# Second-weight remainder loads of a routed feed-forward stage: issued by ScalarE in two halves, instead of by SyncE in four quarters

## The reference

```python
router_probs = softmax(x_flat @ router_w.T)
top_k_probs, top_k_idx = top_k(router_probs, 2)
for e in range(8):
    h = new_gelu(x_flat @ w1[e].T + b1[e])      # 256 -> 1024
    out_e = h @ w2[e].T + b2[e]                 # 1024 -> 256
    output = output + cw[:, e:e + 1] * out_e    # cw: the two weights of a row
```

## Time and profile before

| | |
|---|---|
| median of three executions | 1002.55 us |
| the profiled execution's own time | 1003.09 us |
| its span, first to last instruction | 1001.0 us |
| TensorE matmul busy | 919.7 us (92%) |
| VectorE, ScalarE, GpSimd busy | 574.2, 588.3, 634.2 us |
| mean granted TensorE clock | 0.973 of full speed |
| loads of `w_remainder` | 168 of 256 KB, issued by SyncE |

### The profile page before, as it was taken

One profiled execution on the slowest core, in us unless ns is written; L12 is line 12 of the kernel. 1 busy time (PEld: TensorE's weight loads), 2 busy tenths in 40 slices (PEclk: granted clock), 3 DMA queues, 4 the chain that ended last, 5 costly groups with the idle time before them and its releaser, 6 DMA issues. The chain is left out here.

```text
span 1001.0 us, 21138 instructions
## 1 busy us (share of the span) xinstructions
PE 919.7 (92%) x6800; PEld 838.8 (84%) x6800; DVE 574.2 (57%) x1333; ACT 588.3 (59%) x1242; POOL 634.2 (63%) x632
## 2 busy tenths in 40 slices
PE   6998999999999999799889999987999999999980
PEld 5885777777889988699879999976999999999980
DVE  1547999986766663688543667474333433333334
ACT  0332777776566675587455666524667666766644
POOL 3575888876555554443169988703777777777760
PEclk9999999999999999999999999989999999999995
DMA  8773444441211111000080000183666666666657
GB/s 315 248 258 94 138 158 158 157 141 36 98 47 45 56 64 64 1 1 2 1 344 1 17 16 18 52 333 107 181 196 200 207 191 192 196 209 191 192 178 277
DMA packets 66776, 134.61 MB, mean 134 GB/s; under 512 B 12809, under 2 KB 29364, under 8 KB 65524
## 3 DMA queue, kind: packets, MB, share of 16 engines
q1 hardware_dynamic: 58126, 116.49, 35.6%
q0 software_dynamic: 4032, 11.02, 3.0%
q10 hardware_dynamic: 4550, 6.24, 1.8%
HBM read 111.56 MB, written 23.21 MB: 135 GB/s over the span
## 5 line engine op out<-in xcount | busy, mean ns | idle before, releaser
L122 DVE CAST place<-place 128x512 fp32r<-128x512 f32 (+1 forms) x168 | 88.3, 567 | 155.3 <-PE moe_down L128 98.1
L2590 POOL TENSOR_TENSOR place<-place,place 128x512 fp32r<-128x512 f32 x84 | 138.1, 1644 | 50.2 <-DVE place L122 50.1
L2616 PE MATMUL moe_up<-place,place 128*128 128x128 f32 x1344 | 157.0, 275 | 0.5 <-ACT place L2715 0.5
L2616 PEld LDWEIGHTS moe_up<-place,place 128*128 128x128 f32 x1344 | 153.4, 192 | 0.8 <-ACT place L2715 0.8
L128 PE MATMUL moe_down<-place,place 128*128 128x256 f32 x1008 | 131.1, 286 | 4.4 <-DMA place<-w_remainder 2.5
L128 PEld LDWEIGHTS moe_down<-place,place 128*128 128x128 f32 x1008 | 123.3, 191 | 4.9 <-issue 4.9
L128 PE MATMUL ff_up<-place,place 128*128 128x384 f32 (+2 forms) x540 | 109.4, 345 | 0.1
L2732 ACT ACTIVATE place<-moe_up,place 128x128 f32<-128x128 f32 x336 | 95.4, 367 | 16.9 <-POOL place L2590 12.5
L2719 ACT ACTIVATE place<-place 128x2048 f32 x42 | 80.3, 1914 | 22.4 <-issue 13.1
L128 PEld LDWEIGHTS ff_up<-place,place 128*128 128x128 f32 x540 | 89.1, 193 | 4.5 <-POOL place L1794 0.4
L1779 POOL TENSOR_TENSOR place<-place,place 128x384 fp32r<-128x384 f32 x42 | 43.7, 1043 | 67.3 <-ACT place L1584 44.8
(11 more groups left out here) (323 smaller groups left out, 1954.3 us busy)
## 6 DMA issues: line engine op xcount, KB each, us to landing
place<-w_remainder SPq DMA_DIRECT2D x168, 256.0 KB, 3.8
place<-in_w_dram SPq DMA_DIRECT2D x4, 4096.0 KB, 13.4
place<-gate_rows SPq DMA_DIRECT2D x24, 384.0 KB, 4.8
place<-in_w_dram SPq DMA_DIRECT2D x16, 512.0 KB, 3.8
w_remainder<-place SPq DMA_DIRECT2D x16, 512.0 KB, 2.9
place<-choices SPq DMA_DIRECT2D x5, 768.0 KB, 6.9
place<-value_rows SPq DMA_DIRECT2D x56, 64.0 KB, 2.6
place<-in_patches_dram SPq DMA_DIRECT2D x8, 384.0 KB, 5.3
```

The source lines that it names most:

```text
L122: return eng.tensor_copy(out, x)
L2590: pool.tensor_tensor(lo[f], raw[f], hi[f].bitcast(F32), ALU.subtract).then_inc(h_split, 1)
L2616: last = pe.matmul(p1[u][k // HK][:, (k % HK) * P:(k % HK + 1) * P], ws[u][:, c, k * P:(k + 1) * P], xT[u][:, c, :], start=(c == 0), stop= ...
```

## The change

The two halves for block 0 are issued by SyncE. All later ones are issued by ScalarE, each behind the gelu half of the same number, with a wait for the last matmul of that half in the block before. TensorE waits once for each half instead of once for each quarter. The semaphores of the quarters' ends stay; `quarter_mm[0]` and `quarter_mm[2]` are no longer waited for by anyone.

```diff
-        ... w2_rest_in = ..., sem("moe_w2_rest_in", 4)
+        ... w2_rest_in = ..., sem("moe_w2_rest_in", 2)
...
-                def load_rest(e, q):
-                    sp.dma_start(w2_lo[q // 2][:, (q % 2) * 2:(q % 2) * 2 + 2, :].bitcast(F32),
-                                 self.w2_rest[:, bass.ds(e * KF + q * 2, 2), :]).then_inc(w2_rest_in[q], 16)
-
                 e = owner_of(sp, 0)
-                for q in range(4):
-                    load_rest(e, q)
-                with sp.Fori(0, NBLK - 1) as n:
-                    e = owner_of(sp, n + 1)
-                    for q in range(4):
-                        sp.wait_ge(quarter_mm[q], n + 1)
-                        load_rest(e, q)
-                for q in range(4):
-                    sp.wait_ge(w2_rest_in[q], 16 * NBLK)
+                for f in range(2):
+                    sp.dma_start(w2_lo[f].bitcast(F32), self.w2_rest[:, bass.ds(e * KF + f * HK, HK), :]).then_inc(w2_rest_in[f], 16)
+                for f in range(2):
+                    sp.wait_ge(w2_rest_in[f], 16 * NBLK)
...
-                            if k % 2 == 0:
-                                pe.wait_ge(w2_rest_in[q], n * 16 + 16)
+                            if k == 0:
+                                pe.wait_ge(w2_rest_in[f], n * 16 + 16)
...
+                def load_rest(n, e, f):
+
+                    act.wait_ge(quarter_mm[2 * f + 1], n)
+                    act.dma_start(w2_lo[f].bitcast(F32), self.w2_rest[:, bass.ds(e * KF + f * HK, HK), :]).then_inc(w2_rest_in[f], 16)
+
...
                         for f in range(2):
                             hidden(n + 1, 1 - u, e, f)
+                            load_rest(n + 1, e, f)
                 e = owner_of(act, NBLK - 1)
                 for f in range(2):
                     hidden(NBLK - 1, 1, e, f)
+                    load_rest(NBLK - 1, e, f)
```

More of the change, by code:

```diff
@@ L2490, in routed @@
         ws_ready, up_mm, gl = sem("moe_w1_staged"), sem("moe_up_mm"), sem("moe_gelu", 2)
-        h_cut, h_split, w2_cut, w2_rest_in = sem("moe_hidden_cut"), sem("moe_hidden_split"), sem("moe_w2_cut"), sem("moe_w2_rest_in", 4)
+        h_cut, h_split, w2_cut, w2_rest_in = sem("moe_hidden_cut"), sem("moe_hidden_split"), sem("moe_w2_cut"), sem("moe_w2_rest_in", 2)
         quarter_mm, y_read, stored = sem("moe_quarter_mm", 4), sem("moe_down_read"), sem("choices_stored", 2)
```

## The result

The changed kernel is slower by a little. Over all executions taken side by side for the first comparison its median is 1012.16 us (20 executions) against 1006.15 us for the kernel before (20 executions); the ratio is 1.0044, 95% interval 1.0026 to 1.0063, so about +4.4 us. The two medians lie 6.0 us apart, which is inside that interval (2.6 to 6.3 us) as well. One of the 20 executions of the changed kernel took 2352.13 us, for which nothing here gives a reason, and the ratio leaves it out. Its profiled execution took 1014.72 us, with a span of 1012.7 us. The kernel before is at 1006.15 us here and not at the 1002.55 us of the three executions that the prediction started from; over all runs of this document one execution of it lies anywhere between 1000 and 1014 us.

What follows compares the result with a forecast made beforehand. TensorE's gapless matmuls, 6.66 us a block, were taken as the bound. 0 (40 blocks) + 0 (ScalarE) + 0.3 (end) = +0.3 us on the profiled 1003.09; with the median at 1002.55, forecast 1002.9 us, range 1001.0 to 1009.

Steps and rivals of the forecast that it cites:

- What bounds the stage: Routed stage: TensorE's matmuls fill each block of 6.66 us without a gap, so no faster other engine shortens it.
- Issue times and need times: Block loop: half 0 issued at about 809.1, needed at 813.90; half 1 at 810.55 and 815.35; cover 4.8 us each.
- Time that a half takes: Block loop: 512 KB lands in 4.0 us (half 0) or 4.3 (half 1), below the cover; 40 blocks cost 0 us.
- Rival 1: TensorE's wait ahead of each half: landing over 4.8 us, at the high end 0.34 us a block, 14 us; chance 0.17.
- ScalarE: ScalarE's two issues per block: its work comes later, but nothing is late for an engine TensorE waits for; 0 us.
- The end: `fall(41)` directly behind `fall(40)`, without cover: starts 0.5 us later, partly hidden; +0.3 us, bounds 0 and +1.0.
- SyncE's free time wins nothing: Issuing loads from another engine saves only the issuing sequencer's time; SyncE's is free, so nothing is won.

Runs made afterwards that it cites:

- run 20: Not a label of a run: part of "run 20 times", the unchanged kernel before, executed 20 times in the first comparison; median 1006.15 us.
- The dose: Changed kernel, but ScalarE issues both halves at the end of `fall`, behind both gelu halves; ratio 1.0249 (1.0212 to 1.0286).
- the two-buffer kernel: Changed kernel with a second buffer for both halves of w2_lo, loads issued earlier, second biases and their 1 MB load left out; ratio 1.0003.
- the halves with spread padding: Changed kernel with padding slots scattered to 128 different unused rows of `choices` in place of one; ratio 1.0035, median 1007.56 us.
- their own counterpart: Kernel before (SyncE, quarters) with padding slots scattered to 128 different unused rows of `choices`; ratio 0.9994, median 1002.75 us.

## Why the prediction was wrong

It forecast +0.3 us with a range of 1001.0 to 1009.0 us; measured are +4.4 us and 1012.16 us. About 3.6 us of the miss are no step of the argument: the kernel before is itself at 1006.15 us when it is run 20 times, and I had tied the forecast to three runs. The rest, 4.4 us by the ratio and 6.0 by the medians, is this, as far as the profiles show it.

- *What bounds the stage*: right. Every kernel with quarters has 259.65 us for 39 blocks, whoever issues them.
- *Issue times and need times*: right. Half 0 was issued at 878.3 with the next `fall` due at 883.16, 4.8 us of cover; half 1 had 4.9.
- *Time that a half takes*: this step failed, in its use more than in its middle. "I take 4.0 for half 0 and [...] 4.3 for half 1. Both are below 4.8, so TensorE waits for neither." Measured are 3.7 and 4.5 in the middle, but with a spread of 3.5 to 5.0, so that the upper part of it lies over the cover: 9 to 13 of 39 blocks are longer than 6.70 us in the five profiles with halves, one buffer and these issue times, by 0.04 to 0.7 us each. Nearly all of it is half 1. Rows 5 had a sign of that: the landings pooled there are those of quarters 1 and 2 alone, 3.2 and 4.0 us in the middle, so the second half's first quarter by itself took what I gave to all of half 0. I had written down 4.4 and 5.1 as high ends and then used them only as a rival. A price that is 0 up to a threshold and linear above it has to be summed over the spread. The 40 blocks, costed at 0, cost 1.8 to 2.6 us. Why a half is late in one block and not in the next is shown for about half of that only (the padding).
- *Rival 1* was the right mechanism, at 0.05 to 0.07 us a block and not at the 0.34 that I gave it. The dose (cover 3.3 us, +0.53 us a block) confirms it.
- *ScalarE*: right, 0 us. Its second gelu half moved behind `fall`'s first half as described, and ScalarE with even four issues cost nothing in the steady blocks. An issue took 0.35 us there, not 0.49.
- *The end*: mis-sized. I took +0.3 us, with +1.0 as bound; measured +1.7. I gave half 0 the 4.2 us of quarter 1; it took 4.9 us, and so `fall(41)` starts 1.2 us later in that pair of profiles and not 0.5. The lower clock of `fall(41)` wasn't foreseen at all. Of the time hidden behind the scatters I had 0.4 us; in that pair VectorE's last bias ended 2.7 us later and the last scatter started 2.1 us later, so 0.65 were hidden.
- *SyncE's free time wins nothing*: right, and the Trainium skill's rule in DMA: Bandwidth & Descriptors ("Issuing engines are not separate DMA queues") agrees with the pair of runs in which only the engine changed, 0.9986 (0.9963 to 1.0009). The 3.2 us for 512 KB, an estimate from the fit in that page's section "Anatomy of one DMA — SWDGE (gpsimd) path", is below every landing of a 512 KB load measured here (3.4 us at best, beside other traffic).

At the stage's start the rows turned first came 6.2 to 7.2 us behind the first filler in seven profiles with halves (without the two-buffer kernel, which leaves out a load there and has 5.5), and 5.5 to 6.4 in five with quarters and the same filler. The means are 0.5 us apart; this was only read, not tested.

## What to carry to other kernels

Merging the loads of a single-buffered operand saved issues that cost nothing here, and made the consumer wait for the last byte of a larger piece: compare the slowest landing, not the median one, with the cover, and sum the excess over the blocks. Keep the hand-over in the pieces in which the consumer reads, whoever issues them. When TensorE's wait grows at a place without cover, look at its clock behind it too. And set a variant beside the kernel that shares all else with it: against the kernel before, the halves with spread padding seem to cost 0.1 us at the end, against their own counterpart 1.5.

## What was not expected of the hardware

In the kernels with one buffer an indirect scatter of 128 rows of 1 KB landed in 2.4 us where its rows were different (but for block 0, 2.4 to 4.6 us, and two single ones of 4.3 and 2.9), and in 2.6 to 4.7 us in partly filled blocks with 56 to 126 rows going to one address. It doesn't simply grow with their number: the last two blocks, all 128 rows to one address, took 3.1 to 3.3. Half 0 issued 1.0 to 1.3 us behind such a scatter took 4.5 to 5.3 us in place of about 3.7, but not behind blocks 4 and 16. With padding spread over different rows all scatters from block 1 on landed in 2.4 to 2.5. Repeated rows are not the only thing that goes with a slow scatter: with two buffers, where half 0 is issued 1.45 us ahead of the scatter, all 21 scatters whose landing is recorded (the odd blocks) took 4.3 to 4.9 us but the last, 3.1, full blocks too. TensorE's granted clock fell to the 1.2 GHz level behind short idle times, but not each time. At the stage's start this is so in 7 of the 14 profiles, all with 1.3 to 2.0 us of idle time ahead of the first transpose, and in none of the seven with 0.98 us or less; the first `rise` there took 5.19 us from first to last start in place of 3.56. This is most of the 2.6 us by which the first pair of profiles differs at the stage's start, and it befell three of the six profiles with quarters too. `fall(41)` was at the lower level in 9 of 14, behind 1.8 to 3.9 us of idle time; in the kernel before's first profile 2.50 us left it at 2.4 GHz, and 2.13 us in the one with more filler at the start.
